# A chain of box filters and spectral mixing layers on one core: weights of four layers loaded in one transfer per tensor, and row sums and a root chain in other places of a block

## What is computed

```
def _block(x, ln1w, ln1b, ln2w, ln2b, w1, w2, b1, b2, mw1, mb1, mw2, mb2):
    residual = x
    xn = _ln(transpose(x, (0, 2, 3, 1)), ln1w, ln1b)          # over 64 channels
    xf = rfft2(xn, axes=(1, 2), norm='ortho')
    o1 = relu(complex_matmul(xf, w1) + b1)
    o2 = complex_matmul(o1, w2) + b2
    xc = o2 * (|o2.re| > 0.01 or |o2.im| > 0.01)
    x = residual + transpose(irfft2(xc))
    xp2 = _ln(transpose(x, (0, 2, 3, 1)), ln2w, ln2b)
    h = gelu(xp2 @ mw1 + mb1)
    return x + transpose(h @ mw2 + mb2)
for i in range(4):
    x = _block(x, ...)
```

## Time and profile before

| | us |
|---|---|
| three runs | 3795.04, 3796.38, 3802.16 |
| median | 3796.38 |
| the profiled execution's own time | 3798.83 |
| its span, first to last instruction | 3796.9 |
| PE busy | 3299.8 (87%) |
| DVE busy | 2437.3 (64%) |
| ACT busy | 2377.3 (63%) |
| POOL busy | 1713.5 (45%) |

### The profile page before, as it was taken

How to read it: one execution, slowest core, us unless ns; L and a number is a source line. 1 busy time by engine, 2 the same in 40 slices (tenths; PEclk the granted TensorE clock), 3 DMA queues, 4 the chain that set the end, 5 groups by cost and what they waited for, 6 DMA issues and landing times. The chain is left out here.

```text
span 3796.9 us, 54132 instructions
## 1 busy us (share of the span) xinstructions
PE 3299.8 (87%) x18664; PEld 2009.6 (53%) x18664; DVE 2437.3 (64%) x4175; ACT 2377.3 (63%) x3944; POOL 1713.5 (45%) x1397
## 2 busy tenths in 40 slices
PE   2951879999999999898999999999999999777479
PEld 0641746555565646464646464646555565255247
DVE  1843675767676667676766667575757655369567
ACT  0852566667676757676766666666657665547358
POOL 2404445445555554545445454545545533234232
PEclk9985989999999999999999999999999999989779
DMA  9871111111111111213121111111101111263798
GB/s 226 251 249 60 45 50 40 56 39 62 45 45 50 45 45 45 111 45 133 45 84 45 50 40 51 40 50 45 62 29 62 45 45 51 58 263 117 186 261 245
DMA packets 235117, 334.15 MB, mean 88 GB/s; under 512 B 38624, under 2 KB 163680, under 8 KB 228720
## 3 DMA queue, kind: packets, MB, share of 16 engines
q1 hardware_dynamic: 198112, 298.44, 23.2%
q10 hardware_dynamic: 28784, 18.44, 2.1%
q0 software_dynamic: 7968, 13.99, 1.5%
HBM read 183.99 MB, written 146.80 MB: 87 GB/s over the span
## 5 line engine op out<-in xcount | busy, mean ns | idle before, releaser
L1507 ACT ACTIVATE a_hidden<-a_wide,a_up_b 128x1024 f32<-128x1024 f32 x512 | 569.8, 1113 | 136.4 <-PE a_wide L1683 135.0
L1683 PE MATMUL a_wide<-a_yc,a_up_fold 64*128 64x512 f32 x2048 | 583.5, 645 | 52.8 <-ACT a_hidden L1507 48.5
L1694 PE MATMUL a_result<-a_hidden,a_down 128*64 128x512 f32 x2048 | 516.1, 625 | 67.4 <-DVE a_x L1364 66.0
L1259 POOL TENSOR_TENSOR a_y<-a_o,a_mag 128x256 f32<-128x256 f32 (+1 forms) x512 | 365.4, 739 | 385.6 <-DVE a_mag L1353 385.6
L1217 POOL TENSOR_TENSOR a_y<-a_x,a_stat 128x512 f32<-128x512 f32 x256 | 267.9, 1047 | 483.8 <-DVEq L1398 463.6
L1336 DVE TENSOR_TENSOR a_o<-a_bank,a_mix_b 128x512 f32<-128x512 f32 (+1 forms) x272 | 181.6, 668 | 278.4 <-PE a_bank L1640 274.3
L1520 ACT ACTIVATE a_delta<-a_result,a_down_b 128x512 f32<-128x512 f32 x256 | 176.3, 689 | 263.6 <-PE a_result L1694 263.5
L1658 PEld LDWEIGHTS a_bank<-a_dft_h,a_g 128*128 128x128 f32 x2080 | 272.4, 191 | 129.0 <-issue 129.0
L1640 PEld LDWEIGHTS a_bank<-a_mix,a_o 128*128 128x128 f32 x2080 | 252.8, 191 | 150.8 <-issue 132.9
L1205 POOL TENSOR_TENSOR a_x<-a_x,a_odd 128x512 f32<-128x512 f32 (+1 forms) x128 | 161.2, 1259 | 367.9 <-DVE a_x L1306 298.2
L1364 DVE TENSOR_TENSOR a_x<-a_result,a_x 128x512 f32<-128x512 f32 x256 | 176.1, 688 | 225.5 <-PE a_result L1709 223.3
(11 more groups left out here) (191 smaller groups left out, 6370.1 us busy)
## 6 DMA issues: line engine op xcount, KB each, us to landing
a_x<-rows SPq DMA_DIRECT2D x112, 512.0 KB, 4.5
rows<-a_x SPq DMA_DIRECT2D x112, 512.0 KB, 2.9
box_x<-in_x SPq DMA_DIRECT2D x64, 256.0 KB, 4.3
turned<-box_o SPq DMA_DIRECT2D x64, 256.0 KB, 3.6
a_y<-turned SPq DMA_DIRECT2D x16, 1024.0 KB, 11.0
box_x<-rows SPq DMA_DIRECT2D x16, 1024.0 KB, 24.1
turned<-box_work SPq DMA_DIRECT2D x64, 256.0 KB, 2.0
box_x<-turned SPq DMA_DIRECT2D x64, 256.0 KB, 3.8
```

What stands on the lines that cost most here:

```text
L1259: ins = G.tensor_tensor(y[n % 2][:, :, to].rearrange("p c k -> p k c"), o2[:, j % 3, lo:4, r], mask[:, lo:4], ALU.mult)
L1507: A(hidden[:, i % 2, j], wide[:], ACT.Gelu, bias=up_b2[:, l, j:j + 1]).then_inc(s_hid, 1)
L1683: mm = M(wide[:, half * BANK:(half + 1) * BANK], up_fold[cs, l, j * P:(j + 1) * P], yc[cs, i % 2], start=True, stop=True)
L1694: mm = M(result[half * C:(half + 1) * C, :], down[:, l, j, :], hidden[:, i % 2, j, half * BANK:(half + 1) * BANK], start=j == 0, stop=j == ...
```

## The change

There are two edits that have nothing to do with each other.

**Weights.** Before, each layer had 22 loads of its own and a semaphore of its own. Now there are 25 loads, each with all four layers of a tensor, and one semaphore, for whose full count DVE waits ahead of the first layer.

```
-N_WLOAD = 22
+N_WLOAD = 25
-        s_w = [sem(f"w{i}") for i in range(L)]
+        s_w = sem("w")
...
                 for l in range(L):
-                    dve.wait_ge(s_w[l], 16 * N_WLOAD)
+                    if l == 0:
+                        dve.wait_ge(s_w, 16 * N_WLOAD)
...
-                    for l in range(L):
-                        loads = []
-                        for t, n in ((mix1, "w1"), (mix2, "w2")):
-                            for i in range(2):
-                                for j in range(2):
-                                    loads.append((t[i * C:(i + 1) * C, l, j * C:(j + 1) * C], w[n][l, (i + j) % 2]))
...
-                        loads.append((mix2_b[:, l], w["b2"][l].rearrange("r c -> (r c)").partition_broadcast(P)))
...
-                        for o, i in loads:
-                            act.dma_start(o, i).then_inc(s_w[l], 16)
+                    loads = []
+                    for t, n in ((mix1, "w1"), (mix2, "w2")):
                         for i in range(2):
+                            for j in range(2):
+                                loads.append((t[i * C:(i + 1) * C, :, j * C:(j + 1) * C],
+                                              w[n][:, (i + j) % 2].rearrange("l c d -> c l d")))
+                    for t, n in ((ln1, "ln1"), (ln2, "ln2")):
+                        for i in range(2):
+                            loads.append((t[i * C:(i + 1) * C, :, 0], w[n + "_w"].rearrange("l c -> c l")))
+                        loads.append((t[0:C, :, 1], w[n + "_b"].rearrange("l c -> c l")))
+                    for i in range(2):
+                        loads.append((mix1_b[i * C:(i + 1) * C, :], w["b1"][:, i].rearrange("l c -> c l")))
+                    for i in range(2):
+                        loads.append((up[i * C:(i + 1) * C], w["mlp_w1"].rearrange("l c q -> c l q")))
+                    for j in range(HC):
+                        loads.append((up_b[:, :, j], w["mlp_b1"][:, j * P:(j + 1) * P].rearrange("l p -> p l")))
+                        loads.append((down[:, :, j], w["mlp_w2"][:, j * P:(j + 1) * P].rearrange("l p c -> p l c")))
+                    for i in range(2):
+                        loads.append((down_b[i * C:(i + 1) * C, :], w["mlp_b2"].rearrange("l c -> c l")))
+                    loads.append((mix2_b[:].rearrange("p l q -> p (l q)"),
+                                  w["b2"].rearrange("l r c -> (l r c)").partition_broadcast(P)))
+                    assert len(loads) == N_WLOAD
+                    for o, i in loads:
+                        act.dma_start(o, i).then_inc(s_w, 16)
```

```
-                        if s == (3 if q in (5, 12) else 1):
-                            for strip in strips_at(n, q):
+                        if s == (3 if q == 5 else 1):
+                            for strip in (strips_at(n, 12)[1:] if q == 13 else []) + strips_at(n, q)[:1]:
                                 sum_up(*strip)
                         if FIRST_ROOT <= r < END_ROOT:
-                            if q in (1, 13) and s == 1:
+                            if q == 1 and s == 1:
                                 root(r, range(ROOT_STEPS))
-                            if (q, s) in ((5, 3), (9, 2)):
+                            if (q, s) in ((5, 3), (9, 2), (13, 2)):
                                 root(r, range(ROOT_STEPS // 2))
-                            if (q, s) in ((6, 1), (9, 3)):
+                            if (q, s) in ((6, 1), (9, 3), (14, 1)):
                                 root(r, range(ROOT_STEPS // 2, ROOT_STEPS))
...
-                        act.wait_ge(s_sq_read, i)
+                        act.wait_ge(s_sq_read, i - ((kind, u) == (2, 1) and in_mag(r, 1, 1) and has_second(r + 1)))
...
+                    if q == 12:
+                        for strip in strips_at(n, q)[:1]:
+                            square(*strip)
...
                     if q == 12:
-                        for strip in strips_at(n, q):
+                        for strip in strips_at(n, q)[1:]:
                             square(*strip)
```

More of the change, by code:

```diff
@@ L1436, in _ @@
+                    for t, n in ((mix1, "w1"), (mix2, "w2")):
                         for i in range(2):
-                            loads.append((up[i * C:(i + 1) * C, l], w["mlp_w1"][l]))
-                        loads.append((up_b[:, l], w["mlp_b1"][l].rearrange("(j p) -> p j", p=P)))
-                        loads.append((down[:, l], w["mlp_w2"][l].rearrange("(j p) c -> p j c", p=P)))
+                            for j in range(2):
+                                loads.append((t[i * C:(i + 1) * C, :, j * C:(j + 1) * C],
+                                              w[n][:, (i + j) % 2].rearrange("l c d -> c l d")))
@@ L1440, in _ @@
+                    for t, n in ((ln1, "ln1"), (ln2, "ln2")):
                         for i in range(2):
-                            loads.append((down_b[i * C:(i + 1) * C, l:l + 1], w["mlp_b2"][l].rearrange("(c a) -> c a", a=1)))
-                        assert len(loads) == N_WLOAD
-                        for o, i in loads:
-                            act.dma_start(o, i).then_inc(s_w[l], 16)
+                            loads.append((t[i * C:(i + 1) * C, :, 0], w[n + "_w"].rearrange("l c -> c l")))
+                        loads.append((t[0:C, :, 1], w[n + "_b"].rearrange("l c -> c l")))
```

## The result

The changed kernel takes 3758.78 us in the median of 4 runs (3755.65 to 3759.8), the kernel before 3799.2 in the same round. The ratio is 0.9893, 95% interval 0.9876 to 0.991: 40.4 us faster. The forecast was 3756 us, 40.6 us faster. The span of the profiled execution is 3753.8 us.

The account below looks back on a forecast made before the run. It took TensorE's standing still to bound the kernel: waits for `residual` and the start of L1. 19 us plus 21.6 us gave 40.6, so 3758.2 profiled and 3756 for the median, range 3744 to 3770.

Parts of the forecast that it names:

- Weights land at W = 288: Start of L1: weight and raw-image queues are served packet for packet, so the last weights land at 288 us.
- The Trainium skill's whole packets: Start of L1, rival: raw loads hardly delay the weights, W = 270, 18 us more gained, 3738; chance 0.13.
- The rival of issues that cost by their elements: Start of L1: issues with four times the elements cost four times as much, part one loses 9 us, 3784; chance 0.06.
- Folds in one piece, first sum at 301.7: Start of L1: four folds take 12.0 us behind the weights; first sum at 301.7 instead of 320.76, 19 us gained.
- First strip's sums hidden with 0.5 us to spare: Block 12: two reductions, 2.3 us, fit into VectorE's 2.92 us of idling ahead of the third inverse step.
- First wait gone, second 2.3: Run's end: TensorE's `mlp_down` no longer waits for the first `residual`, but still some 2.3 us for the second.
- The root late by 1.5 and `turn` waits for POOL: Run's end: root ready at 1573.6, not 1572.2; POOL's `normalise` follows later, giving back 1.0 to 1.3 of 3.4 us.
- A run like 5: End of a run whose second `residual` wait is followed by a lower TensorE clock: 2.4 us gained, in 8 of 15 runs.
- one like 2: End of a run whose second `residual` wait is 1.40 us and whose `mlp_down` stays at 1.94: 0.75 us gained, 4 runs.
- The terms of the sum: Run ends: 8 x 2.4 + 4 x 0.75 + 2 for the last, 0 at image changes, less 2.6 before run 0: 21.6 us.
- The clock: Run's end: if TensorE's granted clock still falls behind a wait, it falls into the waits for POOL.
- the root's delay eating all: Run's end, rival: POOL's work comes so late that `turn` gains nothing, leaving only 19 us, 3777; chance 0.15.

Follow-up runs that it names:

- second_image_late: The changed kernel with SP loading the second raw image only when all weights have landed: 3746.6 us, against 3794.36 for the kernel before.
- late_fold: The changed kernel with VectorE scaling weights behind the first root chain and taking folded ones behind the second: 3754.59 us, against 3794.36 for the kernel before.
- root_whole: The changed kernel with block 13's root chain in one piece again, the moved sums kept: 3772.82 us, against 3797.35 for the kernel before.
- root_first: The changed kernel with the root's second half ahead of block 14's reductions, not behind them: 3737.18 us, against 3797.35 for the kernel before.

## Why the prediction was right

- *Weights land at W = 288*, 36.7 us behind the first issue. Measured 36.2. The reason, that as many weight packets go as raw ones until the raw loads are through, is shown by the counts above (994 and 989, 216 and 212) and by `second_image_late`. Its sizes were rough, and two errors cancel: there were 7840 weight packets, 1392 fewer than before and not 384, but what was left of them behind the raw loads took longer than I had for it. For `second_image_late` it gave 24.5 us, and 26.4 were measured. The Trainium skill's whole packets, "DMA: Bandwidth & Descriptors", section "Queues, rings and completion order", would have landed them 19 us behind the first issue: the trace does not agree with what I drew from it. The equal counts don't tell whether one packet or several of each queue go in turn. The rival of issues that cost by their elements is out: two loads of `mlp_w1`, with four times the elements, take 1.31 us, and took 1.12.
- *Folds in one piece, first sum at 301.7*, so 19 us gained. Measured 19.7. The last weights landed 28.6 us sooner (36.2 behind the first issue, not 64.8). Of this 8.9 went to the folds, 9 as worked out, and `late_fold` showed the folds to be on the path.
- *First strip's sums hidden with 0.5 us to spare.* 0.55 was left.
- *First wait gone, second 2.3.* 2.54 gone, 2.35 left.
- *The root late by 1.5 and `turn` waits for POOL.* Counted from the third inverse step, the root ended 1.2 later (15.97 us behind it, not 14.77) and `residual` of block 13 came 4.5 sooner. There were two waits of 1.19 and 1.42, where I had about 1.5 each. A run like 5 gained 2.6 us (2.4 predicted), one like 2 gained 0.97 (0.75).
- *The terms of the sum.* Counted at the same matmul of TensorE in both traces, from the first sum on, 2.5 us were lost ahead of run 0 (2.6 predicted). The eight ends like run 5's gained 20.7 (19.2), the four like run 2's 3.9 (3), the last 3.1 (2). The two at a change of images lost 4.5, for which I took 0. That term was mis-sized: I named the stage fill that waits for `next_y`, but gave it no price. It cancels in part against the others, which gave more, and 20.6 us are left for a predicted 21.6. So the closeness of the sum is in part luck.
- *The clock.* I let it fall into the waits for POOL at no cost. In this change that holds, as runs with and without a fall are alike at 178.1. It failed as a rule in `root_whole`, and in `root_first`, where a run with a fall takes 1.5 us more than one without.
- The total is 40.4 for a predicted 40.6, but the stretches ahead of and behind L1 scatter by some 7 us each from profile to profile, so the last three us of the agreement say nothing.

Of the rivals, *the root's delay eating all* was wrong in size only. The delay is real: `root_first` takes it away and wins 21.4 us to the last `residual`. But it took less than the moved sums and halves gave: 20.6 us were left.

## What to carry to other kernels

When a wait is cut short by moving work to the front of a queue, look at what that work's neighbours release next: here `residual` came 4.5 us sooner, but the root behind it 1.2 later, and POOL passed that on. Two lines that put the root first gave half as much again as the whole change. In a start where many small loads are issued, ask who else is loading, and what stands behind the last one in one piece. Where TensorE waits a few us at a time, bringing all such waits down together may give more than their sum, because the clock stays up.

## What the runs showed that I had not expected

- VectorE's small scalings beside POOL's tensor operations took 2.2 to 2.9 us instead of 0.19 to 0.35, as long as the POOL operation that they met. Its reductions and its reads of PSUM took no longer (1.22 us at 316.33 and 0.29 at 311.52 in `late_fold`, each beside a POOL operation of 2.8). The Trainium skill, "SBUF — State Buffer", section "Who interferes with whom", says that these two engines share one pair of ports as an exclusive lock, so that one of them stands still while the other holds it. The trace agrees: 2.82 us beside POOL's 2.78, 0.19 alone.
- After 4.14 us of idling TensorE's granted clock was 0.50 for 4 us, which cost more than a root that was ready sooner gave. After idling of 2.35 us it fell in some runs (0.72 over 6 us) and not in others (1.94 us for the same matmuls right behind it). With no wait over 0.82 us it did not fall in the run looked at.
- Two DMA queues with work waiting each moved the same number of packets in 4 us (216 and 212), though the raw loads' packets held some 7 KB each and the weights' some 0.2 KB.
- The time ahead of L1, in code that no kernel here changes, was 247.0 to 253.9 us.
